# A software-pipelined transformer block on one core: three column-strip products made neighbours, the key product moved ahead of them, the output product moved into the next slot

## The chip, the cores and the metric

One core of a Trainium2 chip runs the whole program. The metric is the device time of one execution in microseconds. Three timed runs of the kernel before gave 581.37, 579.84 and 581.23 us (median 581.23). One more execution was profiled; it took 578.15 us, of which 576.3 us are the span that the trace covers. TensorE's granted clock was 0.996 of full speed over that span.

## The reference, cut to what matters

The input is 32 sequences ("batches" here) of 128 tokens and 128 features, with a conditioning vector each. Everything is float32.

```
y      = clip(modulated_linear(x))                      # per batch
q,k,v  = y@Wq (16 heads of 64), y@Wk, y@Wv (4 groups)
A      = softmax(q k^T / 8) v ;  x1 = x + y + A@Wpost   # attention over 128 tokens
kx     = modulated_linear(x1)  -> 16 heads of 8
mix    = softmax(kx kx^T / sqrt(8)) kx                  # per token, over its 16 heads
tok    = modulated_linear(mix)
out    = x1 + mixture_of_8_experts(tok)                 # top 2, experts over capacity are dropped
```

## The kernel before, in words

The program is written engine by engine; each engine has its own instruction list and waits on semaphores for the others. The first stage, attention and head mixing, is a software pipeline over the 32 batches. It runs in *slots*: in slot s every engine does a part of several batches: a = s+1 (queries, keys, values, the first scores), s (transposed scores, exponentials, denominators, attended values), c = s-1 (output projection of the attention, the key product of head mixing), h = s-2 (head scores), d = s-3 (mixing and its output product). Slots 4 to 29 are a hardware loop over pairs of slots; slots -2 to 3, 30 and 31 and the three drain slots are unrolled. After that comes the mixture of experts, which the change doesn't touch.

The order of the work within a slot is written out by hand in `loop_slot` for TensorE and VectorE, in `slot` for ScalarE and GpSimd. An engine works strictly down its list, so an instruction that waits holds up all that is behind it. All accumulators in PSUM are shared between stages: `bank_s` takes the scores of one head group after the other (`scores`, read by VectorE's `heads_max`) and then their transposed negative maxima; `bank_t` the transposed scores, which ScalarE turns into `prob`; `bank_d` the attention's projection (`posts`) and then the softmax denominators; `bank_a[1]` the key product and its turn (`keys`, `keys_turned`) and then the second half of the attended values (`attend(s, j, 1)`); `misc[1]` the second half of the queries and then mixing (`mixing_turned`, `tokens_made`).

Three products use TensorE in column strips of 32: `denominators` (L687) and the two halves of `attend` (L695). Each issues four matmuls of 512 columns, which the trace shows as eight, because a float32 product goes through in two passes. They work on four strips of the array side by side; the trace writes such a shape as 128*32. The transposed scores (L672, L677) use two row halves of the array (64*128), everything else the whole array.

TensorE's order in a slot is: first half of the queries, transposed maxima (L812), first half of the projection, transposed scores 0 and 1 (L672, L677), keys and values, second half of the projection, transposed scores 2 and 3, scores 0 (L662), `keys`, second half of the queries, scores 1, denominators, the next batch's `y` product (L864), `attend` 0, `keys_turned` (L790), scores 2, `attend` 1, `mixing_turned` (L795), scores 3, `tokens_made` (L799). `attend` 1 waits for ScalarE's `keys_twice` (`kx`), which empties `bank_a[1]`. `tokens_made` waits for ScalarE's `mixing_out` (`mixT`).

VectorE keeps the row maxima of the scores (L300), the normalisation of the attended values by `inv_den` (`normalise`, L308), the residual sum (`attended`, L460), and the head mixing: `weight_sums` (L437), `weighted_rows` (`mix_lo`, L447), `row_sum` (L454), `head_scores` (L407), `head_shift` (L413, L418). GpSimd multiplies `pair` (L1360, the head scores' products), scales `xs` (L1332), adds `y` to `x` (L1344) and does the other half of the mixing, `mix_hi` (product L1348, three sums L1355). All ScalarE instructions have line L1001; they are told apart by their tiles. ScalarE's two copies that mirror the head scores (`head_copies`, the tile `score`) exist before the change too.

## Time and profile before

| | |
|---|---|
| timed runs | 579.84 to 581.37 us, median 581.23 |
| profiled execution | 578.15 us, its span 576.3 us |
| busy share of the span | TensorE 91%, VectorE 70%, ScalarE 70%, GpSimd 53% |
| of 50 to 470 us (420 us) | TensorE 386.7 us busy, VectorE 311.7, ScalarE 309.4, GpSimd 252.2 |
| DMA | 7.2 MB in all, nearly all of it in the first and last 30 us |

The starts of the first transposed-score product of each slot (L672) stand 14.1 to 14.4 us apart from slot 4 on. Starts and durations in a timeline are in microseconds from the start of the span. Matmuls overlap: a product's printed duration holds its way through the array, so the cost of one that isn't waiting is the distance from its start to the next start, and idle time before a matmul is counted from a modelled end. The same holds, by about 0.1 us, for VectorE and ScalarE, whose successive instructions overlap by that much where they don't depend on each other.

### The profile page before, as it was taken

What the parts mean: (1) busy time and instruction counts of PE and PEld (TensorE: products, weight loads), DVE (VectorE), ACT (ScalarE), POOL (GpSimd) and SP (SyncE); (2) the same over time, 40 slices, a digit from 0 to 9 for tenths busy, and PEclk for the clock granted to TensorE, in tenths of its full rate; (3) what the DMA queues carried; (4) which work ended last, traced back from release to release, by engine and by line L of the source; (5) the groups of instructions that cost most, each with busy time, mean ns of one, the idle gap of its engine ahead of it and who ended that gap; (6) DMA issues with size and microseconds to landing.
All of it is one profiled execution on the core that took longest, in us unless ns stands there. A gap on an engine that the chain in (4) does not pass through costs nothing.

```text
span 576.3 us, 12883 instructions
## 1 busy us (share of the span) xinstructions
PE 524.4 (91%) x3896; PEld 349.0 (61%) x3896; DVE 403.7 (70%) x715; ACT 402.9 (70%) x911; POOL 303.6 (53%) x268
## 2 busy tenths in 40 slices
PE   7999999999999999999999999999999987978997
PEld 7755555555556556565656565655565665655665
DVE  4234777777777777777777777777777767962866
ACT  3667677777777777777777777777777644656783
POOL 1002666666666666666666666666666544600951
PEclk9999999999999999999999999999999999999999
DMA  7400000000000000000000000000000000000004
GB/s 237 100 2 2 1 2 0 1 1 0 0 0 0 0 0 0 0 0 0 0 0 0 0 0 0 0 0 0 0 0 0 1 2 0 1 1 2 1 1 146
DMA packets 9365, 7.20 MB, mean 12 GB/s; under 512 B 1088, under 2 KB 8832, under 8 KB 9216
## 3 DMA queue, kind: packets, MB, share of 16 engines
q1 hardware_dynamic: 9344, 6.94, 4.0%
q8 instruction: 11, 0.18, 0.1%
q14 instruction: 10, 0.08, 0.0%
HBM read 4.84 MB, written 2.10 MB: 12 GB/s over the span
## 4 chain that ended last, share of the span: by engine, by line
PE 67%; ACT 17%; issue 8%; DVE 5%; DMA 1%; ACTq 1%; SPq 1%; POOL 0%; DVEq 0%; POOLq 0%
PE misc L702 11%; PE bank_d L710 10%; PE bank_t L677 10%; PE bank_a L695 5%; PE bank_t L947 4%; PE bank_t L672 4%; PE misc L826 3%; ACT inv_den L1001 3%; ACT log_den L1001 3%; PE bank_s L662 3%; PE misc L799 2%; ACT q L1001 2%; PE misc L828 2%; PE bank_s L955 2%; ACT kx L1001 2%
## 5 line engine op out<-in xcount | busy, mean ns | idle before, releaser
L1360 POOL TENSOR_TENSOR pair<-kx 128x1152 f32<-128x1152 f32 x32 | 82.4, 2575 | 182.9 <-DVE shifted L418 165.1
L300 DVE TENSOR_REDUCE row_max<-bank_s 128x4 bf16<-128x512 f32 x128 | 88.5, 691 | 52.0 <-PE bank_s L662 52.0
L695 PE MATMUL bank_a<-prob,v 128*32 128x512 f32 x512 | 68.1, 604 | 24.6 <-ACT kx L1001 24.6
L1355 POOL TENSOR_TENSOR mix_hi<-mix_hi 128x512 f32<-128x512 f32 (+2 forms) x96 | 80.5, 838 | 7.5
L1001 ACT ACTIVATE prob<-bank_t 128x512 f32<-128x512 f32 x128 | 69.5, 594 | 21.4 <-PE bank_t L677 21.4
L1348 POOL TENSOR_TENSOR mix_hi<-weight,kx 128x1024 f32<-128x1024 f32 x32 | 76.7, 2397 | 0.0
L710 PE MATMUL bank_d<-attT,wpost_sb 128*128 128x128 f32 x512 | 70.6, 282 | 0.1
L702 PE MATMUL misc<-yT,wq_sb 128*128 128x128 f32 x512 | 69.1, 278 | 0.7 <-DVE yT L489 0.7
L710 PEld LDWEIGHTS bank_d<-attT,wpost_sb 128*128 128x128 f32 x512 | 65.8, 195 | 2.1 <-issue 0.3
L677 PE MATMUL bank_t<-qT,kT 64*128 64x256 f32 x512 | 65.7, 376 | 0.0
L702 PEld LDWEIGHTS misc<-yT,wq_sb 128*128 128x128 f32 x512 | 62.2, 192 | 3.5 <-issue 2.0
L454 DVE TENSOR_REDUCE mix_part<-mix_lo 128x128 f32<-128x1024 f32 x32 | 63.0, 1968 | 0.3
L677 PEld LDWEIGHTS bank_t<-qT,kT 64*128 64x128 f32 x512 | 49.3, 189 | 4.9
L460 DVE TENSOR_TENSOR x_all<-bank_d,x_all 128x128 f32 (+1 forms) x32 | 9.3, 291 | 59.7 <-PE bank_d L710 59.7
L662 PE MATMUL bank_s<-k,q 128*128 128x256 bf16 x256 | 49.3, 274 | 0.5 <-ACT q L1001 0.3
L1001 ACT ACTIVATE qT<-misc 128x512 f32<-128x512 f32 x64 | 38.1, 595 | 14.0 <-PE misc L702 13.9
L407 DVE TENSOR_REDUCE score<-pair 128x144 f32<-128x1152 f32 x32 | 43.0, 1342 | 2.5 <-POOL pair L1360 2.5
L447 DVE TENSOR_TENSOR mix_lo<-weight,kx 128x1024 f32<-128x1024 f32 x32 | 44.4, 1387 | 0.0
L308 DVE TENSOR_TENSOR attT<-bank_a,inv_den 128x512 f32<-128x512 f32 x64 | 43.4, 679 | 0.0
L1001 ACT ACTIVATE q<-qT 128x512 bf16<-128x512 f32 x64 | 40.3, 629 | 1.1
L1001 ACT ACTIVATE neg_diag<-bank_s 128x512 bf16<-128x512 f32 x32 | 19.1, 597 | 30.6 <-PE bank_s L812 30.6
L662 PEld LDWEIGHTS bank_s<-k,q 128*128 128x128 bf16 x256 | 24.7, 109 | 15.9 <-issue 10.8
(182 smaller groups left out, 954.9 us busy)
## 6 DMA issues: line engine op xcount, KB each, us to landing
out<-acc_all SPq DMA_DIRECT2D x8, 256.0 KB, 2.3
x_all<-in_xT SPq DMA_DIRECT2D x1, 1024.0 KB, 9.3
w_sb<-in_w SPq DMA_DIRECT2D x2, 512.0 KB
x_all<-in_xT SPq DMA_DIRECT2D x1, 768.0 KB, 7.0
wq_sb<-in_wq SPq DMA_DIRECT2D x1, 512.0 KB, 5.4
wpost_sb<-in_wpost SPq DMA_DIRECT2D x1, 512.0 KB, 9.5
x_all<-in_xT SPq DMA_DIRECT2D x1, 256.0 KB, 3.3
b_rows<-in_b SPq DMA_DIRECT2D x16, 4.0 KB
```

Of the source, the lines that this page charges most:

```text
L300: V.tensor_reduce(bass.AP(row_max, first_w * (P + 1) + HPG * p, [[HPG * P, P], [P + 1, 2], [KEY, 2], [1, 1]]), bank_s[:, :, :].rearrange(" ...
L447: V.tensor_tensor(mix_lo[:, :, :].rearrange("p r (h e) -> p r h e", e=MD), weight[:, jd, 0:MH // 2, :].unsqueeze(3).to_broadcast([P, MH // ...
L454: V.tensor_reduce(mix_part[:, :], mix_lo[:, :, :].rearrange("p r f -> p f r"), AX.X, ALU.add).then_inc(s_lo, 3)
L662: last = mm(bank_s[:, 2 * w:2 * w + 2, :], q16[:, j, g // 2, g % 2 * 2 + w, :], k16[:, j, g // 2, :, :], start=(w == 0), stop=True, skip_g ...
L677: last = mm(bank_t[half][:, w:w + 2, :], kT[rows, j, p, :], qT[rows, j, p, w:w + 2, :], start=False, stop=True, skip_group_check=True)
L695: last = mm(bank_a[part][rows, :], v[:, j, g, 32 * part:32 * (part + 1)], prob[:, g, :, :], start=True, stop=True, skip_group_check=True)
L702: last = mm(bank[:, c % 4, :], wq_sb[:, c * P:(c + 1) * P], yT[:, :], start=(c % 4 == 0), stop=True, skip_group_check=True)
L710: last = mm(bank_d[:, 0, :], wpost_sb[:, k, :], attT[:, k, :], start=(k == 0), stop=(k == CHUNKS - 1))
L1001: return nc.scalar.activation(out_, in_, func, **kw)
L1348: G.tensor_tensor(mix_hi[:, jd, :, :].rearrange("p r (h e) -> p r h e", e=MD), weight[:, jd, MH // 2:MH, :].unsqueeze(3).to_broadcast([P, ...
L1355: G.tensor_tensor(mix_hi[:, jd, 0:r, :], mix_hi[:, jd, 0:r, :], mix_hi[:, jd, r:2 * r, :], ALU.add).then_inc(s_hi, 1)
L1360: G.tensor_tensor(pair[:, :, :], bass.AP(kx2, jc * 2 * P, [[4 * P, P], [0, SHIFTS], [1, P]]), bass.AP(kx2, jc * 2 * P, [[4 * P, P], [MD, S ...
```

## The change

It only reorders. No instruction is added or taken away, and no shape changes.

- TensorE: `keys` goes ahead of transposed scores 2 and 3, `keys_turned` ahead of scores 1, and the `y` product ahead of the denominators, so that denominators, `attend` 0 and `attend` 1 are neighbours. Scores 3 go to the next slot, behind the first half of the queries; `tokens_made` goes to the next slot, behind them. The second half of the projection goes up to right behind the transposed maxima.
- VectorE: `heads_max(.., 3)` and the second `normalise` go to the head of the next slot; `attended` ahead of `head_scores`; `heads_max(a, 1)` behind the mixing sums; `yT` ahead of the first `normalise`.
- ScalarE: the first half of the queries is copied ahead of `neg_diag`; `tokens_out` goes to the next slot, and `x1_scaled` directly behind it, ahead of the exponentials; `keys_out` ahead of `v`; `head_copies` ahead of the second half of the queries; `keys_twice` and `y` ahead of its narrowing and of the two denominator instructions, `log_den` and `inv_den`.

```diff
--- before
+++ after
@@ -462,2 +462,6 @@
                 def loop_slot():
+                    if B:
+                        heads_max(s, 3)
+                    if C:
+                        normalise(c, 1)
                     if D:
@@ -465,7 +469,5 @@
                         weighted_rows()
-                    head_scores()
                     if C:
                         attended()
-                    if A:
-                        heads_max(a, 0)
+                    head_scores()
                     if D:
@@ -473,3 +475,3 @@
                     if A:
-                        heads_max(a, 1)
+                        heads_max(a, 0)
                     if D:
@@ -477,9 +479,5 @@
                     mixed(mix_part[:, :])
-                    head_shift()
                     if A:
-                        heads_max(a, 2)
-                    if s_is(s, BATCH - 1):
-                        count_ahead()
-                    if B:
-                        normalise(s, 0)
+                        heads_max(a, 1)
+                    head_shift()
                     if has(a + 1):
@@ -489,5 +487,9 @@
                         V.tensor_scalar(yT[:, :], misc[0][:, 1, :], CLAMP, -CLAMP, ALU.min, ALU.max).then_inc(s_yT, 1)
-                    if A:
-                        heads_max(a, 3)
+                    if s_is(s, BATCH - 1):
+                        count_ahead()
                     if B:
+                        normalise(s, 0)
+                    if A:
+                        heads_max(a, 2)
+                    if s_is(s, BATCH - 1):
                         normalise(s, 1)
@@ -809,2 +811,10 @@
                     if B:
+                        scores(s, j, 3)
+                    if has(d - 1):
+                        tokens_made(d - 1)
+                    if C:
+                        if isinstance(s, int) and c == 0:
+                            pe.wait_ge(s_ld_post, 32)
+                        posts(c, 0)
+                    if B:
                         pe.wait_ge(s_max, 4 * n(s))
@@ -815,5 +825,3 @@
                     if C:
-                        if isinstance(s, int) and c == 0:
-                            pe.wait_ge(s_ld_post, 32)
-                        posts(c, 0)
+                        posts(c, 1)
                     if s_is(s, 0):
@@ -829,6 +837,6 @@
                            stop=True, skip_group_check=True).then_inc(s_kv_mm, 1)
-                    if C:
-                        posts(c, 1)
                     if final:
                         gate_logits(parts_early[1])
+                    if C:
+                        keys(c)
                     if B:
@@ -840,4 +848,2 @@
                         scores(a, ja, 0)
-                    if C:
-                        keys(c)
                     if A:
@@ -849,10 +855,7 @@
                         gate_logits(parts_early[2])
+                        gate_logits(parts_early[3])
+                    if C:
+                        keys_turned(c)
                     if A:
                         scores(a, ja, 1)
-                    if final:
-                        gate_logits(parts_early[3])
-                    if B:
-                        if C:
-                            pe.wait_ge(s_x1T, n(c))
-                        denominators(s)
                     if s_is(s, -1):
@@ -865,8 +868,6 @@
                     if B:
+                        if C:
+                            pe.wait_ge(s_x1T, n(c))
+                        denominators(s)
                         attend(s, j, 0)
-                    if C:
-                        keys_turned(c)
-                    if A:
-                        scores(a, ja, 2)
-                    if B:
                         if C:
@@ -881,5 +882,3 @@
                     if A:
-                        scores(a, ja, 3)
-                    if D:
-                        tokens_made(d)
+                        scores(a, ja, 2)
                     if final:
@@ -891,2 +890,3 @@
                     if s == BATCH:
+                        tokens_made(d - 1)
                         posts(c, 0)
@@ -1131,3 +1131,3 @@
 
-                def mixing_out():
+                def mixing_out(d):
                     act.wait_ge(s_mixT_mm, n(d))
@@ -1137,3 +1137,3 @@
 
-                def tokens_out():
+                def tokens_out(d):
                     act.wait_ge(s_o_mm, n(d))
@@ -1145,2 +1145,3 @@
                     if s == BATCH:
+                        tokens_out(d - 1)
                         copy_logits(EARLY, 4)
@@ -1157,5 +1158,5 @@
                         ahead(0, 1, 2)
-                        mixing_out()
+                        mixing_out(d)
                         ahead(3)
-                        tokens_out()
+                        tokens_out(d)
                     if s == BATCH + 1:
@@ -1164,10 +1165,10 @@
                         ahead(5, 6)
-                        mixing_out()
+                        mixing_out(d)
                         ahead(7)
-                        tokens_out()
+                        tokens_out(d)
                     if s == BATCH + 2:
                         ahead(8)
-                        mixing_out()
+                        mixing_out(d)
                         ahead_keep(9)
-                        tokens_out()
+                        tokens_out(d)
                         ahead_relu(11)
@@ -1181,2 +1182,5 @@
                     return
+                if A:
+                    copy_q(a, ja, 0)
+                    narrow_q(a, ja, 0)
                 if B:
@@ -1185,5 +1189,6 @@
                     f(neg_diag[:, j, :, :], bank_s[:, :, :], scale=-1.0).then_inc(s_neg, 1)
-                if A:
-                    copy_q(a, ja, 0)
-                    narrow_q(a, ja, 0)
+                if has(d - 1):
+                    tokens_out(d - 1)
+                if C:
+                    x1_scaled()
                 if B:
@@ -1199,2 +1204,5 @@
                         f(k16[rows, ja, :, half, :], misc[0][rows, 0:2, :]).then_inc(s_k16, 1)
+                if C:
+                    keys_out()
+                if A:
                     need(act, s_av_mm, 2 * n(a - 2))
@@ -1202,4 +1210,2 @@
                       misc[0][:, 2:4, :].rearrange("p a (g e) -> p (a g) e", e=KEY)).then_inc(s_v, 1)
-                if C:
-                    x1_scaled()
                 if B:
@@ -1207,2 +1213,3 @@
                     exp_scores(s, 3)
+                head_copies()
                 if A:
@@ -1210,8 +1217,3 @@
                 if C:
-                    keys_out()
-                if A:
-                    narrow_q(a, ja, 1)
-                if B:
-                    invert_den(s)
-                head_copies()
+                    keys_twice()
                 if has(a + 1):
@@ -1222,8 +1224,9 @@
                       bias=modb_sb[:, 0:1]).then_inc(s_y_raw, 1)
-                if C:
-                    keys_twice()
+                if A:
+                    narrow_q(a, ja, 1)
+                if B:
+                    invert_den(s)
                 head_weights()
                 if D:
-                    mixing_out()
-                    tokens_out()
+                    mixing_out(d)
```

## Rows read from the trace of the kernel before

**Rows 1.** Timeline of TensorE: start us, us, line, out<-in, [idle before <-releaser].

```profile
252.72 1.06 PE L687 MATMUL bank_d<-prob,ones 128*32 128x512 f32 x8
253.72 0.49 PE L864 MATMUL misc<-xs,modw_sb 128*128 128x128 f32 x2
254.13 1.06 PE L695 MATMUL bank_a<-prob,v 128*32 128x512 f32 x8
...
256.48 1.06 PE L695 MATMUL bank_a<-prob,v 128*32 128x512 f32 x8 [0.80 <-ACT kx L1001]
...
258.37 0.49 PE L799 MATMUL misc<-mixT,modw_sb 128*128 128x128 f32 x2 [0.35 <-ACT mixT L1001]
...
260.86 0.39 PE L672 MATMUL bank_t<-neg_diag,g_rows 64*128 64x512 bf16 x2
...
262.04 0.71 PE L826 MATMUL misc<-yT,wk_sb 128*128 128x128 f32 x4
...
263.02 1.05 PE L710 MATMUL bank_d<-attT,wpost_sb 128*128 128x128 f32 x8
264.01 0.39 PE L672 MATMUL bank_t<-neg_diag,g_rows 64*128 64x512 bf16 x2
```

**Rows 2.** Timeline of TensorE, the last two slots of the pipeline.

```profile
451.98 1.06 PE L687 MATMUL bank_d<-prob,ones 128*32 128x512 f32 x8
452.87 1.04 PE L695 MATMUL bank_a<-prob,v 128*32 128x512 f32 x8
...
459.96 0.39 PE L672 MATMUL bank_t<-neg_diag,g_rows 64*128 64x512 bf16 x2
```

**Rows 3.** Timeline of ScalarE in the same slot as Rows 1.

```profile
262.14 1.09 ACT L1001 ACTIVATE prob<-bank_t 128x512 f32<-128x512 f32 x2 [0.38 <-PE bank_t L677]
263.22 0.38 ACT L1001 ACTIVATE kT<-misc 128x256 f32<-128x256 f32 x1
...
264.69 0.40 ACT L1001 ACTIVATE x1s<-x_all,style 128x128 f32 x1
...
266.74 0.60 ACT L1001 ACTIVATE qT<-misc 128x512 f32<-128x512 f32 x1 [0.36 <-PE misc L702]
...
270.19 0.38 ACT L1001 ACTIVATE kx<-bank_a 128x256 f32<-128x256 f32 x1
```

**Rows 4.** Timeline of VectorE in the same slot.

```profile
258.13 0.69 DVE L300 TENSOR_REDUCE row_max<-bank_s 128x4 bf16<-128x512 f32 x1
258.73 0.68 DVE L308 TENSOR_TENSOR attT<-bank_a,inv_den 128x512 f32<-128x512 f32 x1
259.33 0.57 DVE L437 TENSOR_REDUCE h_den<-weight 128x16 f32<-128x256 f32 x1
259.82 1.50 DVE L447 TENSOR_TENSOR mix_lo<-weight,kx 128x1024 f32<-128x1024 f32 x1
...
264.23 0.29 DVE L460 TENSOR_TENSOR x_all<-bank_d,x_all 128x128 f32 x1 [1.64 <-PE bank_d L710]
...
268.72 0.24 DVE L442 RECIPROCAL h_rden<-h_den 128x16 f32<-128x16 f32 x1
...
269.91 0.58 DVE L413 TENSOR_REDUCE h_max<-score 128x16 f32<-128x256 f32 x1 [0.42 <-ACT score L1001]
270.52 0.43 DVE L418 TENSOR_TENSOR shifted<-score,h_max 128x256 f32<-128x256 f32 x1
```

**Rows 5.** Timeline of GpSimd in the same slot.

```profile
256.90 2.58 POOL L1360 TENSOR_TENSOR pair<-kx 128x1152 f32<-128x1152 f32 x1 [5.29 <-DVE shifted L418]
...
260.20 2.96 POOL L1348 TENSOR_TENSOR mix_hi<-weight,kx 128x1024 f32<-128x1024 f32 x1
```

**Rows 6.** Timeline of GpSimd in the last slot of the pipeline.

```profile
458.77 1.96 POOL L1348 TENSOR_TENSOR mix_hi<-weight,kx 128x1024 f32<-128x1024 f32 x1
460.81 3.47 POOL L1355 TENSOR_TENSOR mix_hi<-mix_hi 128x512 f32<-128x512 f32 x3
```

**Rows 7.** Timeline of VectorE in the last slot of the pipeline.

```profile
458.89 2.92 DVE L447 TENSOR_TENSOR mix_lo<-weight,kx 128x1024 f32<-128x1024 f32 x1
```

More of the change, by code:

```diff
@@ L465, in loop_slot @@
                         weighted_rows()
-                    head_scores()
                     if C:
                         attended()
+                    head_scores()
+                    if D:
+                        row_sum()
                     if A:
@@ L471, in loop_slot @@
                     if D:
-                        row_sum()
+                        weight_inverses()
+                    mixed(mix_part[:, :])
                     if A:
                         heads_max(a, 1)
-                    if D:
-                        weight_inverses()
-                    mixed(mix_part[:, :])
                     head_shift()
-                    if A:
-                        heads_max(a, 2)
-                    if s_is(s, BATCH - 1):
-                        count_ahead()
-                    if B:
-                        normalise(s, 0)
                     if has(a + 1):
@@ L881, in loop_slot @@
                     if A:
-                        scores(a, ja, 3)
-                    if D:
-                        tokens_made(d)
+                        scores(a, ja, 2)
                     if final:
@@ L1210, in slot @@
                 if C:
-                    keys_out()
-                if A:
-                    narrow_q(a, ja, 1)
-                if B:
-                    invert_den(s)
-                head_copies()
+                    keys_twice()
                 if has(a + 1):
@@ L1222, in slot @@
                       bias=modb_sb[:, 0:1]).then_inc(s_y_raw, 1)
-                if C:
-                    keys_twice()
+                if A:
+                    narrow_q(a, ja, 1)
+                if B:
+                    invert_den(s)
                 head_weights()
                 if D:
-                    mixing_out()
-                    tokens_out()
+                    mixing_out(d)
             slots(act, slot)
```

## The prediction

> **What bounds the kernel now.** I read the busy shares first, then the timeline of one slot on each engine, then the chain of waits. TensorE is the busiest engine by far, and in the slot shown it stands idle at two places only: 0.80 us before the second half of `attend`, ended by ScalarE's `kx`, and 0.35 us before `tokens_made`, ended by `mixT` [rows 1]. The chain of waits runs through TensorE for the whole slot except at these two places. So the slot is TensorE's own work plus two waits. From one slot's first L672 to the last slot's there are 14 slots: (459.96 - 260.86)/14 = 14.22 us each [rows 1, 2].
>
> The reader should see three costs in TensorE's rows. First the two waits. Second, switching between strips and the whole array: denominators to the `y` product takes 1.00 us (252.72 to 253.72) and `y` to `attend` 0.41 us for two short passes [rows 1]. In slot 30, which has no `y` product, the same denominators are followed directly by `attend` after 0.89 us [rows 2]. Third, nothing else: after 256.48 the rest is dense.
>
> **The change on TensorE.** No matmul is added or removed.
>
> - Strips in a row: denominators and `attend` 0 each pass to another strip product in 0.89 us instead of 1.00, 0.22 together. The `y` product's 0.41 contains a way back into strips and a weight load that stood open; I put it at 0.25, so 0.16 less. Sum about 0.4 us.
> - `keys` and its turn ahead: between `keys_turned` and `attend` 1 now lie scores 1, `y`, the denominators and `attend` 0 where only scores 2 lay, so `kx` has emptied `bank_a[1]` by then. That takes the 0.80 us wait.
> - `tokens_made` one slot later, behind the queries: the 0.35 us wait goes. `tokens_out` follows it on ScalarE, where it stands behind `neg_diag`.
>
> TensorE's own slot would then be 14.22 - 0.80 - 0.35 - 0.4 = 12.7 us. Idle time is counted from modelled ends, so each wait may be worth 0.1 to 0.2 us more: 12.3 to 12.7. I take this as the floor and not as the forecast, since the change makes new waits.
>
> **The new loop.** Scores 3 of a batch now run at the head of the next slot, and they wait for `heads_max(.., 2)`. On VectorE that one stands behind the first `normalise`, which needs `inv_den`. On ScalarE the two denominator instructions are now almost last. Behind scores 3 TensorE queues tokens, projection, maxima, second half of the projection, and then the transposed scores that start ScalarE's next run of exponentials. That closes a loop through all three engines. I add it up from the start X of the first exponential.
>
> - ScalarE's run, where it should never wait: two exponentials to `kT` 1.08 us (262.14 to 263.22). `kT`, two `k`, `v`: in the old order 1.47 us until `x1s` starts, which itself waited for the residual sum; I take 1.40. Two more exponentials 1.09 less an overlap of 0.10. The remaining nine instructions (second query copy, `kxT`, narrowing, `log_den`, `inv_den`, two mirror copies, `y`, `kx`) are the same nine that run without idle time between 266.74 and 270.57 now: 3.83 us [rows 3]. Sum 7.30 us from X to the end of `inv_den`.
> - VectorE: from there to the start of `normalise` 0.12 (two waits; estimate between the smallest distance seen, 0.03, and the 0.16 at `attended`). `normalise` to `heads_max` 0.60, `heads_max` itself 0.69 [rows 4].
> - TensorE: 0.05 to start, scores 3 take 0.43 to their end (estimate: two matmuls of 256 columns, their load open because they waited), 0.04 back to VectorE.
> - VectorE: `heads_max` 3 then the second `normalise`, 0.60 and 0.68 [rows 4].
> - TensorE: 0.05, then the second half of the projection: 0.99 from its start to L672 (263.02 to 264.01) plus 0.10 for an open load [rows 1].
> - L672 to the next first exponential: 260.86 to 262.14 = 1.28 [rows 1, 3].
>
> 7.30 + 0.12 + 0.60 + 0.69 + 0.05 + 0.43 + 0.04 + 0.60 + 0.68 + 0.05 + 1.09 + 1.28 = 12.93 us. That is above TensorE's floor, so the three-engine loop sets the period.
>
> **What else lies near.** `x1_scaled` now stands in front of the exponentials, so a late residual sum delays all of ScalarE. Its path: second `normalise` 0.60, `h_den` 0.49, `mix_lo`, `attended`, `x1s` [rows 4]. The start of `mix_lo` is wanted at X + 7.30 + 0.12 + 0.60 + 0.69 + 0.05 + 0.43 + 0.04 + 0.60 + 0.60 + 0.49 = X + 10.92. Here GpSimd matters. In the last slot `mix_hi` ran 458.77 to 460.73 and `mix_lo`, wanted at 458.89, ended at 461.81: it took 2.92 us instead of about 1.1, that is, it waited for `mix_hi` to end and then ran 1.08 us [rows 6, 7]. In the slot of rows 5, `mix_lo` started first with 1.50 and `mix_hi` took 2.96 instead of 1.96 [rows 4 to 6]. The one that comes second waits for the whole instruction.
>
> So where is GpSimd at X + 10.92? Scores 0 start at L672 + 1.18 + 0.98 (262.04 to 263.02) + 0.3 for `keys` and the switch + 1.18 for the second transposed pair = L672 + 3.64 = X + 2.36 [rows 1]; `heads_max` 0 at X + 2.8; 0.60; then from `h_rden` to `h_max` 1.19 less 0.42 of idle time, 0.77; `heads_max` 1 0.60; `h_max` to `shifted` 0.61; `shifted` 0.43 [rows 4]: its end at X + 5.8. `pair` follows 0.08 later and `mix_hi` 3.30 us after it (256.90 to 260.20) [rows 5], at X + 9.2, ending at X + 11.15, with the first of its sums 0.08 behind, at X + 11.2 [rows 6]. `mix_lo` comes within `mix_hi`, waits till X + 11.15, ends at X + 12.23. `attended` (overlap 0.08, 0.29 long), 0.17 to `x1s` (264.52 to 264.69), 0.30 more to the exponential [rows 3, 4]: X + 12.91. The two paths tie, and the period stays 12.9 us, with a margin of 0.3 us before the first sum of `mix_hi` would get in ahead of `mix_lo`.
>
> **Moves costed at nothing.** `neg_diag` behind the query copies: the two instructions of 0.6 us [rows 3] end before the maxima come, since these wait for scores 3. `heads_max` 1 behind the mixing sums: it is wanted by scores 2 only, some 3 us later. `yT` is early by the length of the first `normalise`. `tokens_out` and its `misc[1]`: the second query product comes some 6 us after it. If one of these covers goes, its own 0.3 to 0.6 us join the period. The SP queue and all DMAs are untouched; nothing that moves issues one. GpSimd's list is unchanged, only its releases move.
>
> **Sum.** Slots 4 to 31 are 28 slots at 14.22 - 12.93 = 1.29 us: 36 us. The fill is less loaded and the drain is another order of the same work; I take 1 us gained there, with 3 either way. 578.15 - 37 = 541.2 us for an execution like the profiled one. The timed runs before lay 1.7 to 3.2 us above the profiled one; taking 1.8 of that, the forecast is 543 us.
>
> **Rivals.**
>
> - *TensorE is the bound (0.07).* If the loop is 0.3 to 0.6 us shorter than I add it up, TensorE's 12.3 remain: 28 x 1.92 = 54 us, 526 us. For it: I took two open loads and upper ends. Against it: ScalarE's 7.30 us are nearly all read from dense rows.
> - *Sums of `mix_hi` ahead of `mix_lo`, in every slot (0.13).* If `mix_lo` is wanted after X + 11.2, the first sum holds it off. That sum is about half of the three (3.47 less 1.00 of waiting for `mix_lo`) [rows 6, 7], 1.3 us. `mix_lo` then ends at X + 13.6 and the next X comes at X + 14.28. The period is 14.28 against 14.22: with the 1 us of the fill this is no change, 582 us. Every tenth by which `shifted` is later than X + 5.8 adds 2.8 us; from 0.05 us later on, the kernel is slower than before by over 0.3%, at 0.2 later 588 us. It decides at a delay of 0.3 us on the path to `mix_lo`, about the size of my estimates' error. The Trainium skill, "SBUF — State Buffer", section "Who interferes with whom", says that a VectorE instruction with two SBUF inputs and a GpSimd instruction that reads SBUF exclude each other for their whole length, the later one blocking. Rows 4 to 7 agree (2.92 us for 1.1), and by that rule alone, whichever is issued first decides between 12.9 and 14.3 us.
> - *The same in one of the two slots of the loop body (0.13).* The two already differ before. Mean period 13.6: 28 x 0.62 = 17 us, 563 us.
> - *The forecast's case (0.62)*, period 12.7 to 13.3, 533 to 550 us. The rest (0.05) are longer loops of another kind, between 550 and 575.
>
> About 0.3% is what a measurement of this kernel can tell. The 0.13 of the second rival splits into 0.02 faster, 0.06 same, 0.05 slower; one more in a hundred goes to slower. Faster 0.88, same 0.06, slower 0.06. The range 532 to 566 holds the forecast's case and the half-blocked one and leaves out TensorE's floor and the fully blocked loop.
>
> **What would show it.** Right: L687, L695, L695 at distances of 0.89 us; no idle time before L695; a TensorE wait of about half a microsecond ended by `row_max` before scores 3, and a short one ended by `attT` before the second half of the projection; ScalarE without idle time from the first exponential to `inv_den`; `mix_lo` at 1.1 to 1.6 us; L672 some 12.9 us apart. Wrong: `mix_lo` at 2 us or more with `mix_hi`'s sums beside it, an idle ScalarE in front of `x1s`, or TensorE dense with L672 at 12.3.

## The result, and the profile after

The changed kernel takes 537.69 us (median of four runs, 536.6 to 538.42) where the kernel before takes 580.71 (four runs, 579.84 to 581.37): a ratio of 0.926, 95% interval 0.924 to 0.928. The forecast was 543 us, range 532 to 566. The profiled execution took 537.94 us, against the 541.2 that the sum gave for it. One execution of 1719 us of the kernel of experiment 7, and one of 852 us of the kernel before beside experiment 12, are left out of the medians and ratios.

The two profiled executions lie 40.2 us apart. The starts of the first transposed-score product of each slot (L672 before, L674 after) show where that came from. From slot 4 to slot 31 there are 27 distances. They were 14.23 us on average and are (421.78 - 75.52)/27 = 12.82 now: 27 x 1.41 = 38.0 us. The rest after the last of them shrank from 116.3 to 114.3 us, and slot 4 starts 0.1 us earlier. So the gain is the period of the loop.

The page of after, busy shares and clock:

```profile
PE 509.7 (95%) x3896; PEld 359.1 (67%) x3896; DVE 405.6 (76%) x715; ACT 385.1 (72%) x911; POOL 299.8 (56%) x268
...
PEclk9999999999999999999999999999999989989999
```

Every engine has as many instructions as before; they stand in a shorter span. TensorE's idle time in the span fell from 51.9 us (576.3 - 524.4) to 26.4 (536.1 - 509.7), and its busy time by 14.7 us. Now the timeline of TensorE in after, to be held against [rows 1, 2]:

```profile
247.92 1.07 PE L689 MATMUL bank_d<-prob,ones 128*32 128x512 f32 x8
248.80 1.90 PE L697 MATMUL bank_a<-prob,v 128*32 128x512 f32 x16
250.63 0.33 PE L797 MATMUL misc<-ident,mix 128*128 128x128 f32 x1
...
252.38 0.39 PE L664 MATMUL bank_s<-k,q 128*128 128x256 bf16 x2 [0.31 <-DVE row_max L300]
...
254.15 1.16 PE L712 MATMUL bank_d<-attT,wpost_sb 128*128 128x128 f32 x8
255.24 0.39 PE L674 MATMUL bank_t<-neg_diag,g_rows 64*128 64x512 bf16 x2
```

Denominators to `attend` takes 0.88 us, and both halves of `attend` are one run of 16 with nothing in front: the wait for `kx` is gone. So is the wait for `mixT`. In their place stands 0.31 us before scores 3, ended by `row_max`, and the second half of the projection at 254.15, whose weight load waited 0.21 us for `attT`: 1.09 us from there to L674 (255.24), as the sum had it.

ScalarE and VectorE of after in the same slot [rows 3, 4]:

```profile
243.85 1.06 ACT L1001 ACTIVATE prob<-bank_t 128x512 f32<-128x512 f32 x2
...
250.23 0.63 ACT L1001 ACTIVATE inv_den<-log_den 128x512 f32<-128x512 f32 x1
...
256.43 0.40 ACT L1001 ACTIVATE x1s<-x_all,style 128x128 f32 x1 [1.25 <-DVE x_all L460]
256.73 1.06 ACT L1001 ACTIVATE prob<-bank_t 128x512 f32<-128x512 f32 x2
```

```profile
250.95 0.69 DVE L308 TENSOR_TENSOR attT<-bank_a,inv_den 128x512 f32<-128x512 f32 x1 [1.20 <-PE bank_a L697]
251.56 0.69 DVE L300 TENSOR_REDUCE row_max<-bank_s 128x4 bf16<-128x512 f32 x1
252.81 0.70 DVE L300 TENSOR_REDUCE row_max<-bank_s 128x4 bf16<-128x512 f32 x1 [0.56 <-PE bank_s L664]
253.41 0.68 DVE L308 TENSOR_TENSOR attT<-bank_a,inv_den 128x512 f32<-128x512 f32 x1
254.01 0.58 DVE L437 TENSOR_REDUCE h_den<-weight 128x16 f32<-128x256 f32 x1
254.51 1.55 DVE L447 TENSOR_TENSOR mix_lo<-weight,kx 128x1024 f32<-128x1024 f32 x1
255.98 0.28 DVE L460 TENSOR_TENSOR x_all<-bank_d,x_all 128x128 f32 x1
```

And GpSimd [rows 5, 6]:

```profile
249.70 2.58 POOL L1363 TENSOR_TENSOR pair<-kx 128x1152 f32<-128x1152 f32 x1 [4.05 <-DVE shifted L418]
...
253.00 1.97 POOL L1351 TENSOR_TENSOR mix_hi<-weight,kx 128x1024 f32<-128x1024 f32 x1
255.06 3.48 POOL L1358 TENSOR_TENSOR mix_hi<-mix_hi 128x512 f32<-128x512 f32 x3
```

Read these from the end. ScalarE's exponentials at 256.73 don't start 1.28 us behind L674 (255.24) as in [rows 1, 3], but 1.49 behind it. They stand behind `x1s` at 256.43, which waits for `attended` (255.98), which stands behind `mix_lo`. `mix_lo` is wanted at 254.51 and takes 1.55 us. `mix_hi` is at work until 254.97, and the first of its sums starts at 255.06. So the residual sum, and not the transposed scores (L674) alone, sets the next slot's start.

### The profile page after: what moved, and what is told of

It is laid out like the page before. It is cut to its first block, busy times and chain, and to the rows that moved or that the text cites. A ratio compares the mean times of both kernels' runs of the same rounds, so it can differ in the third digit from the quotient of the medians.

```text
span 536.1 us, 12857 instructions
## 1 busy us (share of the span) xinstructions
PE 509.7 (95%) x3896; PEld 359.1 (67%) x3896; DVE 405.6 (76%) x715; ACT 385.1 (72%) x911; POOL 299.8 (56%) x268
## 4 chain that ended last, share of the span: by engine, by line
PE 51%; ACT 16%; DVE 15%; issue 13%; DVEq 1%; ACTq 1%; POOL 1%; POOLq 0%
PE bank_d L712 6%; PE bank_t L679 6%; PE bank_a L697 6%; ACT prob L1001 6%; PE bank_s L664 4%; PE bank_t L947 4%; DVE row_max L300 4%; PE misc L704 4%; PE bank_d L689 3%; PE bank_t L674 2%; DVE attT L308 2%; DVE mix_lo L447 2%; PE bank_s L955 2%; PE bank_d L955 2%; PE bank_a L635 2%
## 5 line engine op out<-in xcount | busy, mean ns | idle before, releaser
L1358 POOL TENSOR_TENSOR mix_hi<-mix_hi 128x512 f32<-128x512 f32 (+2 forms) x96 | 104.9, 1092 | 7.5
L704 PE MATMUL misc<-yT,wq_sb 128*128 128x128 f32 x512 | 67.8, 276 | 0.3 <-DVE yT L487 0.3
L712 PEld LDWEIGHTS bank_d<-attT,wpost_sb 128*128 128x128 f32 x512 | 62.1, 192 | 7.1 <-DVE attT L308 7.1
L1351 POOL TENSOR_TENSOR mix_hi<-weight,kx 128x1024 f32<-128x1024 f32 x32 | 63.0, 1970 | 0.0
L697 PE MATMUL bank_a<-prob,v 128*32 128x512 f32 x512 | 62.4, 606 | 0.0
L454 DVE TENSOR_REDUCE mix_part<-mix_lo 128x128 f32<-128x1024 f32 x32 | 61.4, 1918 | 0.3
L664 PE MATMUL bank_s<-k,q 128*128 128x256 bf16 x256 | 49.6, 275 | 8.1 <-DVE row_max L300 7.6
L447 DVE TENSOR_TENSOR mix_lo<-weight,kx 128x1024 f32<-128x1024 f32 x32 | 47.8, 1495 | 0.0
L697 PEld LDWEIGHTS bank_a<-prob,v 128*32 128x32 f32 x512 | 17.0, 111 | 38.7 <-issue 37.9
L1001 ACT ACTIVATE x1s<-x_all,style 128x128 f32 (+1 forms) x32 | 12.8, 401 | 38.9 <-DVE x_all L460 38.9
L664 PEld LDWEIGHTS bank_s<-k,q 128*128 128x128 bf16 x256 | 19.6, 103 | 27.9 <-ACT k L1001 10.3
```

The lines of the kernel that those rows point to most:

```text
L447: V.tensor_tensor(mix_lo[:, :, :].rearrange("p r (h e) -> p r h e", e=MD), weight[:, jd, 0:MH // 2, :].unsqueeze(3).to_broadcast([P, MH // ...
L454: V.tensor_reduce(mix_part[:, :], mix_lo[:, :, :].rearrange("p r f -> p f r"), AX.X, ALU.add).then_inc(s_lo, 3)
L664: last = mm(bank_s[:, 2 * w:2 * w + 2, :], q16[:, j, g // 2, g % 2 * 2 + w, :], k16[:, j, g // 2, :, :], start=(w == 0), stop=True, skip_g ...
L697: last = mm(bank_a[part][rows, :], v[:, j, g, 32 * part:32 * (part + 1)], prob[:, g, :, :], start=True, stop=True, skip_group_check=True)
L704: last = mm(bank[:, c % 4, :], wq_sb[:, c * P:(c + 1) * P], yT[:, :], start=(c % 4 == 0), stop=True, skip_group_check=True)
L712: last = mm(bank_d[:, 0, :], wpost_sb[:, k, :], attT[:, k, :], start=(k == 0), stop=(k == CHUNKS - 1))
```

## The experiments

Each ratio is against the kernel before, run on the same chip beside it; after stands at 0.926. "Period" is the mean distance of the first L674 (or L672) of a slot, slots 4 to 31: 14.23 before, 12.82 after. X is the start of a slot's first exponential, as in the prediction. "The port" stands for what `mix_lo` on VectorE and `mix_hi` on GpSimd can't have at the same time [rows 4 to 7]. The port path is the one from `shifted` through `pair`, `mix_hi`, `mix_lo`, `attended` and `x1s` to the next exponentials; the other path is the one through `inv_den` and scores 3. Line numbers differ by a few between the kernels.

**1. `mix_hi` held behind `mix_lo`: is the port path the one that binds?** The kernel is after, with GpSimd's `mix_hi` made to wait for `mix_lo` in every slot but the drain's.

```diff
+                    if not isinstance(s, int) or s < BATCH:
+                        pool.wait_ge(s_lo, 4 * d + 1)
```

> The kernel after, with GpSimd's product mix_hi made to wait until VectorE has written mix_lo of the same batch. Theory P (port): in the kernel after the period of 12.84 us is set by mix_lo waiting for the end of mix_hi (254.51 to 254.97), then attended, x1s and the first exponential. With mix_lo alone on the port it ends 0.46 us earlier; the path through inv_den then sets the period, 12.67 us, and the time falls by 28 x 0.17 = 5 us, to about 533. L672 to the first exponential goes from 1.49 to 1.28 us. Theory T (TensorE bounds the slot) and theory I (the path through inv_den bounds it): no change, 537 to 538, or a little slower where mix_hi is now late for the mixing sums.

535.27 us, ratio 0.922 (0.917 to 0.927), period 12.77, where 533 us and 12.67 were expected. The interval overlaps that of after, so the time alone doesn't tell the two apart; the period does. VectorE and GpSimd of this kernel:

```profile
243.04 1.22 DVE L447 TENSOR_TENSOR mix_lo<-weight,kx 128x1024 f32<-128x1024 f32 x1
...
249.09 0.29 DVE L395 TENSOR_TENSOR mix_sum<-mix_part,mix_hi 128x128 f32<-128x128 f32 x1 [0.37 <-POOL mix_hi L1360]
```

```profile
244.34 1.97 POOL L1353 TENSOR_TENSOR mix_hi<-weight,kx 128x1024 f32<-128x1024 f32 x1 [2.30 <-DVE mix_lo L447]
```

`mix_lo` takes 1.22 us instead of 1.55, but the period falls by 0.06 only. The exponentials come 1.28 and 1.37 us behind L674 in turn, so the path through the port is off. What it leaves is the other path, the one through `inv_den`, and that one got longer: the exponentials now start earlier against TensorE's work, from the exponentials to `kT` it is 1.08 and 0.99 us in turn instead of 0.96, and `inv_den` ends at X + 7.15 and X + 7.06 instead of X + 7.01. VectorE's new wait of 0.37 us for the sums of `mix_hi` costs nothing: `normalise`, further down its list, still waits for `inv_den` or the attended values. So the two paths lie 0.06 us per slot apart, the port's the longer: nearly the tie that was forecast.

**2. `mix_hi` and its sums ahead of `xs` and `x + y`: what if a sum gets in first?**

```diff
-                if A:
-                    pool.wait_ge(s_yT, n(a))
-                if has(s + 2):
-                    xs_of(s + 2, j)
-                if A:
-                    G.tensor_tensor(x_all[:, col(a)], x_all[:, col(a)], yT[:, :], ALU.add).then_inc(s_xy, 1)
```

(The same lines follow behind the sums of `mix_hi`.)

> The kernel after, with GpSimd's mix_hi and its three sums put ahead of xs and x+y in its list. mix_hi then starts some 0.8 us earlier and its first sum is issued before mix_lo is wanted. Theory P: mix_lo waits for that sum of 1.3 us instead of for mix_hi, takes 2.2 us instead of 1.55, and the period becomes 13.4 us: about 555 us. Theories T and I: no change, since no engine has more work, 538.

551.53 us, ratio 0.951 (0.946 to 0.956), period 13.41, as expected (13.4). GpSimd and VectorE:

```profile
247.47 1.97 POOL L1345 TENSOR_TENSOR mix_hi<-weight,kx 128x1024 f32<-128x1024 f32 x1
249.53 3.47 POOL L1352 TENSOR_TENSOR mix_hi<-mix_hi 128x512 f32<-128x512 f32 x3
```

```profile
249.75 2.13 DVE L447 TENSOR_TENSOR mix_lo<-weight,kx 128x1024 f32<-128x1024 f32 x1
```

`mix_lo` is wanted 0.22 us behind the start of the first sum and takes 2.13 us: it waits out the rest of that sum. Up to there nothing moved: `inv_den` ends at X + 7.01 and `mix_lo` is wanted at X + 10.66, both as in after. In after it comes 0.55 us ahead of the first sum (254.51 and 255.06). That distance is what stands between the measured kernel and this one.

**3. Scores 3 at the head of the slot.** They run ahead of the first queries.

```diff
+                    if B:
+                        scores(s, j, 3)
                     if A:
                         pe.wait_ge(s_yT, n(a))
                         queries(a, 0)
-                    if B:
-                        scores(s, j, 3)
```

> The kernel after, with scores 3 ahead of the first half of the queries on TensorE, so that the 0.9 us of queries no longer lie in the shadow of the wait for row_max but behind it. Theory I (the path inv_den, normalise, heads_max, scores 3, heads_max, normalise, projection is within 0.2 us of the bound): the projection comes 0.7 us later, the period grows by 0.5 us to 13.3, about 551 us. Theory T (only TensorE's amount of work counts): no change, 538.

553.6 us, ratio 0.954 (0.949 to 0.959), period 13.39, as expected (13.3). TensorE:

```profile
262.47 0.39 PE L664 MATMUL bank_s<-k,q 128*128 128x256 bf16 x2 [1.27 <-DVE row_max L300]
```

The wait for `row_max`, 0.31 us in after, is 1.27 without the queries in front, and the queries then come late for what follows. What ends the wait doesn't move: `heads_max` 2 stands behind `normalise`, and that behind `inv_den`. The exponentials follow L674 by 1.28 and 1.37 us here, so the port path is off, and this is the loop of the prediction, seen from its TensorE end.

**4. The strips torn apart again.** Scores 2 run between the two halves of `attend`.

```diff
                         attend(s, j, 0)
+                    if A:
+                        scores(a, ja, 2)
+                    if B:
                         if C:
                             pe.wait_ge(s_kx2, n(c))
                         attend(s, j, 1)
...
-                    if A:
-                        scores(a, ja, 2)
```

> The kernel after, with scores 2 put back between attend 0 and attend 1, so that the strips are two in a row and one apart. TensorE pays one more way out of and into strips, some 0.2 to 0.3 us a slot. Theory L (the loop through all engines bounds, TensorE has 0.5 us of waits a slot): the extra cost shortens the wait for row_max before scores 3, no change, 537 to 539 us. Theory T: 28 x 0.25 = 7 us more, 545 us.

538.77 us, ratio 0.930 (0.925 to 0.935), period 12.83: no change that can be told from after. TensorE:

```profile
262.37 1.04 PE L697 MATMUL bank_a<-prob,v 128*32 128x512 f32 x8
263.34 0.39 PE L664 MATMUL bank_s<-k,q 128*128 128x256 bf16 x2
263.66 1.07 PE L697 MATMUL bank_a<-prob,v 128*32 128x512 f32 x8
```

Two more switches between strips and the whole array cost 0.24 us: from the first `attend` to the mix's turn are 264.66 - 262.37 = 2.29 us with scores 2 among them; in after it is 250.63 - 248.80 = 1.83, and scores 2 are 0.22 more (250.80 to 251.02 there). They are paid out of TensorE's wait before scores 3, which has gone in this trace. In the kernel as changed, having strips side by side gives nothing of itself.

**5. ScalarE's second narrowing behind the denominators.** It moves behind `log_den` and `inv_den`, so that these come earlier.

```diff
-                if A:
-                    narrow_q(a, ja, 1)
...
+                if A:
+                    narrow_q(a, ja, 1)
```

> The kernel after, with ScalarE's narrowing of the second half of the queries behind the two denominator instructions, so that inv_den ends 0.52 us earlier. Theory P (port): mix_lo is then wanted earlier but still waits for the end of mix_hi, which depends on shifted and pair only; the period stays 12.8 us and the time 537 to 539. Theory I (the path through inv_den sets the period): 0.4 to 0.5 us less a slot, 524 to 527 us.

537.25 us, ratio 0.925 (0.921 to 0.929), period 12.83: no change. `inv_den` ends 0.52 us earlier (X + 6.49), and the period doesn't follow. TensorE and VectorE:

```profile
252.39 0.38 PE L664 MATMUL bank_s<-k,q 128*128 128x256 bf16 x2
```

```profile
241.46 1.73 DVE L447 TENSOR_TENSOR mix_lo<-weight,kx 128x1024 f32<-128x1024 f32 x1
...
254.52 1.58 DVE L447 TENSOR_TENSOR mix_lo<-weight,kx 128x1024 f32<-128x1024 f32 x1
```

Not all of the 0.52 us reaches `mix_lo`. Scores 3 (L664 at 252.39) no longer wait for `row_max`, but TensorE's own row gets to them no sooner, so `mix_lo` is wanted at X + 10.39 instead of 10.58 in one slot, and at X + 10.65, as in after, in the other. Where it is wanted earlier it takes longer (1.73 us for 1.55), because it waits for the same end of `mix_hi`. So what comes off the path through `inv_den` is worth nothing: the port path binds alone.

**6. Both, 1 and 5.** The edit is that of 1 and that of 5.

> Both edits together: mix_hi waits for mix_lo, and the narrowing stands behind the denominators. If the two paths (port, and inv_den) are in parallel and each near 12.8 us, neither edit alone gives much and both together give the 0.52 us: period 12.77 - 0.42 = 12.35, where TensorE's own work begins to bound, about 523 us. If one of the two paths was no bound at all, the result is that of the better single edit, 535 us.

531.34 us, ratio 0.913 (0.909 to 0.916), period 12.67 (12.54 and 12.80 in turn). It is the fastest kernel of the study, 6.3 us under after, but the 523 us expected weren't reached: they took TensorE's floor, 12.35 a slot. No idle time of a matmul set is left between 100 and 420 us that another engine ends. Three rows of the slot of 12.80 us, and two of the waits of that stretch (what waited, for what: us in total, times, longest):

```profile
248.50 0.33 PE L797 MATMUL misc<-ident,mix 128*128 128x128 f32 x1
248.85 0.39 PE L664 MATMUL bank_s<-k,q 128*128 128x256 bf16 x2
249.32 1.15 PE L704 MATMUL misc<-yT,wq_sb 128*128 128x128 f32 x8
```

```profile
PEld bank_s L664 <- ACT q L1001: 4.6, 24, 0.2
PEld misc L704 <- issue: 3.9, 11, 0.4
```

L797 to scores 2 takes 0.35 us (0.31 in the other slot), 0.17 in after (250.63 to 250.80): with the narrowing behind the denominators, the weight load of scores 2 waits for `q`, 24 times. Scores 2 to the queries takes 0.47 us, 0.22 in after; no data is late, and it comes 11 times, in every second slot, where the loop body of two slots begins anew. In after both lie in front of a wait for `row_max` and cost nothing. The 0.25 us is the difference of the two slots (12.80 and 12.54), and 12.54 less some 0.17 for `q` is near the 12.35. That these two make up the miss is read from the rows; no kernel without them was run.

**7. From the kernel before, the tokens alone one slot later.**

```diff
+                    if has(d - 1):
+                        tokens_made(d - 1)
                     if B:
                         pe.wait_ge(s_max, 4 * n(s))
...
-                    if D:
-                        tokens_made(d)
```

(`tokens_out` on ScalarE moves likewise, behind `neg_diag`.)

> The kernel before, with tokens_made and tokens_out of a batch one slot later and nothing else. The wait for mixT (0.35 us and an open load of 0.11) goes from TensorE's row. Theory S (in the kernel before each TensorE wait adds to the slot): 28 x 0.46 = 13 us less, about 568 us. Rival: kx is then as late as before against an earlier TensorE and the wait before attend 1 grows by the same amount: no change, 580.

577.08 us, ratio 0.995 (0.991 to 0.998), where 568 was expected; the distances are 14.03 us, but for the last (15.45). The wait for `mixT` [rows 1] is gone; another one is there:

```profile
255.29 1.06 PE L695 MATMUL bank_a<-prob,v 128*32 128x512 f32 x8 [0.80 <-ACT kx L1002]
...
257.07 1.16 PE L702 MATMUL misc<-yT,wq_sb 128*128 128x128 f32 x8 [0.24 <-DVE yT L489]
```

```profile
256.14 0.68 DVE L308 TENSOR_TENSOR attT<-bank_a,inv_den 128x512 f32<-128x512 f32 x1
256.74 0.28 DVE L489 TENSOR_SCALAR yT<-misc 128x128 f32<-128x128 f32 x1
```

Without the tokens in front, the queries start 1.78 us behind `attend` 1 instead of 2.22 (256.48 to 258.70 before), and by the row would start 0.24 us earlier still: `yT` stands behind `heads_max` 2 and `normalise` on VectorE, and is ready 1.73 us behind `attend` 1 in both kernels.

**8. The same with `yT` ahead of the first `normalise`.**

```diff
-                    if B:
-                        normalise(s, 0)
                     if has(a + 1):
                         dve.wait_ge(s_y_raw, n(a + 1))
...
+                    if B:
+                        normalise(s, 0)
```

> The kernel before with tokens_made one slot later, as in tokens_alone, and VectorE's yT ahead of the first normalise, as in the kernel after. In tokens_alone the queries then waited 0.24 us for yT, which stood behind heads_max 2 and that normalise. Theory S2 (the wait for mixT was exchanged for the wait for yT): with yT 0.6 us earlier the slot loses the whole 0.46 us, period 13.75, about 567 us. Rival (something else holds the slot at 14.03): no change against tokens_alone, 576.

562.77 us, ratio 0.971 (0.966 to 0.975), period 13.62, somewhat better than expected (567 us, 13.75). One of TensorE's waits is left between 100 and 420 us:

```profile
PE bank_a L695 <- ACT kx L1002: 18.5, 23, 0.8
```

That is 14 us more than 7 from one instruction's place: in the change, the new place of `yT`, which the prediction had put among the moves at nothing, is a condition for the gain of the tokens. The earlier `yT` without the later tokens wasn't run; in the kernel before no matmul waits for `yT`. The wait for `kx` that is left, 0.80 us, is what still lies between this kernel and after: 13.62 - 12.82 = 0.80.

**9. From the kernel before, strips alone.** The denominators move behind the `y` product, so that these and `attend` 0 are neighbours.

```diff
-                    if B:
-                        if C:
-                            pe.wait_ge(s_x1T, n(c))
-                        denominators(s)
...
+                    if B:
+                        if C:
+                            pe.wait_ge(s_x1T, n(c))
+                        denominators(s)
                     if B:
                         attend(s, j, 0)
```

> The kernel before, with the y product ahead of the denominators, so that denominators and attend 0 are neighbours. TensorE saves 0.11 + 0.16 us a slot there, but its next wait, for kx before attend 1, is behind it. Theory W (the saved time is lost in that wait, and the denominators are 0.2 us later for ScalarE): no change, 579 to 584 us. Theory T (fewer changes between strips and the whole array give their time): 7 us less, 573 us.

585.67 us, ratio 1.008 (1.005 to 1.011): slower, where no change was expected (579 to 584 us). TensorE:

```profile
246.59 1.06 PE L695 MATMUL bank_a<-prob,v 128*32 128x512 f32 x8 [1.25 <-ACT kx L1001]
```

The wait for `kx` [rows 1] grew from 0.80 to 1.25 us and took all that the switches gave, and 0.1 us more: the distances are 14.24 and 14.50 in turn, before 14.13 and 14.38. The 0.1 us is ScalarE's: the denominators come later, `inv_den` ends at X + 7.32 instead of 7.21, and `kx` stands behind it. Beyond that, three of the 31 distances were 15.87 us, see the last section.

**10. After, with the tokens back in their own slot.**

```diff
-                    if has(d - 1):
-                        tokens_made(d - 1)
...
+                    if D:
+                        tokens_made(d)
```

(`tokens_out` likewise.)

> The kernel after with tokens_made at the end of its own slot again. TensorE waits 0.5 us for mixT there, and the queries and scores 3 come 0.4 us later than the wait for row_max ends now. The path through inv_den, scores 3 and the second normalise grows by 0.37, to 12.67 + 0.37 = 13.04 us; the port path stays at 12.84. About 543 us. If the later slot of the tokens were worth its whole wait, 12.84 + 0.6: 554 us; if nothing, 538.

557.94 us, ratio 0.961 (0.957 to 0.964), where 543 was expected; distances of 13.96 and 13.35 in turn. VectorE and GpSimd show why:

```profile
252.09 1.22 DVE L447 TENSOR_TENSOR mix_lo<-weight,kx 128x1024 f32<-128x1024 f32 x1
...
265.44 2.27 DVE L447 TENSOR_TENSOR mix_lo<-weight,kx 128x1024 f32<-128x1024 f32 x1
```

```profile
252.20 3.59 POOL L1355 TENSOR_TENSOR mix_hi<-mix_hi 128x512 f32<-128x512 f32 x3
...
265.36 3.47 POOL L1355 TENSOR_TENSOR mix_hi<-mix_hi 128x512 f32<-128x512 f32 x3
```

In one slot `mix_lo` starts 0.11 us ahead of the first sum and takes 1.22; in the next it is wanted 0.08 behind it and takes 2.27. It is wanted at X + 11.02 and X + 11.33 in turn, where after has X + 10.58 and X + 10.66; the expectation had given 0.37 us of delay to the path through scores 3 and none to the race. From exponential to exponential it is 13.04 and 14.30 us. This is the half-blocked loop of the prediction's third rival (12.93 and 14.28), with its period (13.6) and nearly its time (563).

**11. After, with the `y` product between the denominators and `attend` 0.** The denominators move ahead of it.

```diff
+                    if B:
+                        if C:
+                            pe.wait_ge(s_x1T, n(c))
+                        denominators(s)
...
                     if B:
-                        if C:
-                            pe.wait_ge(s_x1T, n(c))
-                        denominators(s)
                         attend(s, j, 0)
```

> The kernel after with the y product between the denominators and attend 0, where it was before. Its switches cost TensorE 0.27 us, as much as in scores2_between, which changed nothing. But the product ends 0.6 us later, and on ScalarE y stands in front of the narrowing, log_den and inv_den. Theory Q (it is the queue on ScalarE that counts): those three are 0.5 us later, period 13.2 to 13.3, 548 to 551 us. Theory W (a TensorE slot has room for it, nothing else matters): 538 us.

576.19 us, ratio 0.991 (0.988 to 0.994), period 14.10; 548 to 551 was expected. ScalarE, VectorE and GpSimd:

```profile
256.44 0.43 ACT L1002 ACTIVATE misc<-misc,modb_sb,demod 128x128 f32<-128x128 f32 x1 [0.49 <-PE misc L871]
```

```profile
262.13 2.28 DVE L447 TENSOR_TENSOR mix_lo<-weight,kx 128x1024 f32<-128x1024 f32 x1
```

```profile
262.06 3.47 POOL L1359 TENSOR_TENSOR mix_hi<-mix_hi 128x512 f32<-128x512 f32 x3
```

The copy of `y` waits 0.49 us with the denominators queued behind it, `inv_den` ends at X + 7.61 instead of X + 7.01, and `mix_lo` falls 0.07 us behind the first sum, now in both slots. 0.6 us of delay became 1.3 us of period. From exponential to exponential it is 14.14 and 14.21 us: the second rival (14.28).

**12. The same with the edit of 1.** The edits are those of 11 and of 1: without the port, is only the delay left?

> y_between with one edit more: GpSimd's mix_hi waits for mix_lo, as in lo_first. In y_between inv_den came 0.60 us later than in the kernel after, and the period grew by 1.3 us. Theory P2 (the delay itself costs some 0.55 us a slot, and the rest is that mix_lo now comes 0.07 us behind the first sum of mix_hi and waits 1.2 us for it): with the order on the port fixed the period is 12.77 + 0.55 = 13.3 us, about 550 us, 26 us less than y_between. Rival (the whole 1.3 us comes from ScalarE's and TensorE's queues): 574 to 576 us, no change against y_between.

553.52 us, ratio 0.955 (0.952 to 0.958), period 13.34, as expected (13.3; the time is 3.5 us above the 550); `mix_lo` takes 1.21 us. So 0.76 of the 1.28 us that 11 lost per slot are the lost race for the port, and 0.52 are the delay of `inv_den`. TensorE waits up to 0.6 us for `row_max` in this kernel, so the two more switches that the `y` product costs it there don't show in the period.

## Why the prediction was right

**The three-engine loop.** It closed as described, and the marks named for "right" are in the rows of after; only the wait for `row_max` is 0.31 us where about half a microsecond was named. One mark named for "wrong" is there too: ScalarE stands idle in front of `x1s`, 1.25 us, where it didn't before [rows 3]. The mark tells less than it was meant to: the idle time is 1.98 and 2.07 us in the blocked loop of experiment 11, but with the port path off (experiment 1) it is still 0.90 and 0.99. The terms of the loop came out so: ScalarE's run 7.01 us (250.86 - 243.85) where 7.30 was summed, the one term that was over-sized by more than 0.1; `inv_den` to `normalise` 0.09 for 0.12; `normalise` to `heads_max` 0.61 for 0.60; the projection 1.09 for 1.09. With 1.28 us from L674 to the exponentials, where the port path made it 1.49, these terms give 12.88 - 0.21 = 12.67 us. With the port path off in truth (experiment 1) it is 12.77, since ScalarE's run is 7.15 and 7.06 us there. So the sum of 12.93 was 0.16 too long, by ScalarE's term.

**The port path.** It was summed at 12.91 and is 12.88 in this slot, and it is the one that binds; the sum called it a tie. Its points against X: end of `shifted` 5.71 (5.8 forecast), `mix_hi` 9.15 (9.2), its first sum 11.21 (11.2), `mix_lo` wanted 10.66 (10.92) and ended 12.21 (12.23). Experiment 5 ends `inv_den` 0.5 us earlier and gains nothing; experiment 1 takes the port off and gains 0.06 us per slot, since the other path then holds. The over-sized 7.30 did the forecast no harm: as long as `mix_lo` comes within `mix_hi`, the port path doesn't depend on that term. It did make the margin ahead of the first sum 0.3 us; it is 0.55. With a margin of 0.3 the two blocked loops looked nearer than they were.

**The rivals.** TensorE as the bound didn't come; even experiment 6, where no matmul set stands idle for another engine, has 12.67 us and not 12.3. (It reached the 12.7 that the prediction had worked out first.) The fully and the half-blocked loop didn't come in after, but experiments 11 and 10 are these two, with periods near those forecast for them (14.10 and 13.63, against 14.28 and 13.6). Each came of one product put elsewhere on TensorE, which took 0.6 us of the margin ahead of the first sum (from 0.55 us ahead to 0.07 and 0.08 behind). The Trainium skill, "SBUF — State Buffer", section "Who interferes with whom", has the later of the two instructions block for the whole length of the other. The rows agree: 1.21 to 1.22 us alone, 1.55 behind the rest of `mix_hi`, 2.13 to 2.28 behind nearly the whole of a sum.

**The strips.** The floor of 12.7 counted 0.4 us for fewer switches: that term has no part in the result. The distances came as read (0.88), but in after they shorten only an engine that waits anyway (experiment 4), and from the kernel before they went into a longer wait for `kx` (experiment 9). The gain is that of the two waits removed. The tokens' part of it (experiment 8, 13.62 against 14.23) needs the earlier `yT` (experiment 7). The part of `kx` wasn't run alone; it is read from the difference of 0.80 us that is left between experiment 8 and after, which is as long as the wait.

**Moves costed at nothing.** None was run alone, but in after the only wait of a matmul between 100 and 420 us is that for `row_max`, and `neg_diag` itself waits 0.73 us for the maxima, so none shows a cost. The exception is `yT`, whose earlier place was worth 0.4 us per slot to the queries.

**Fill and drain.** 1 us was taken, 2.1 was gained; 27 distances and not 28 lie between slots 4 and 31. Of the 5.3 us between the forecast of 543 and the measured 537.69, 3.3 are the sum's (541.2 against 537.94). The other 2 are the step from a profiled execution to the timed ones: 1.8 us was added for it, and this time the timed median lies 0.25 us under the profiled execution.

## What to carry to other kernels

Add up every loop that passes through several engines from one instruction's start back to its own next start, and do it to the second one too: the distance from the longest path to the second is all that you gain by mending the longest (0.06 us a slot in experiment 1). Where two engines exclude each other, ask which of the two instructions comes first and by what margin, since half a microsecond of delay anywhere ahead of it can cost more than twice itself. When an edit removes a wait, look at what the engine asks for next and where that stands in its own queue: here one instruction's place was worth 14 us.

## What was not expected of the hardware

**The clock of TensorE in experiment 9.** Windows of that kernel from 262 to 268 us, the columns: length, busy share and count of TensorE, weight loads, VectorE, ScalarE, GpSimd, then the granted clock:

```profile
262.00:263.00 1.00, 0.65 (x8) 0.29 (x4) 1.00 (x4) 0.38 (x2) 1.00 (x1) 1.00 0.00 0
263.00:264.00 1.00, 1.00 (x5) 1.00 (x6) 1.00 (x3) 0.15 (x1) 1.00 (x1) 0.54 0.00 0
264.00:265.00 1.00, 1.00 (x7) 1.00 (x7) 1.00 (x2) 0.30 (x1) 1.00 (x4) 0.50 0.00 0
...
266.00:267.00 1.00, 1.00 (x8) 0.95 (x7) 1.00 (x1) 0.97 (x3) 1.00 (x1) 0.76 0.00 0
267.00:268.00 1.00, 1.00 (x12) 0.78 (x10) 0.18 (x1) 0.60 (x1) 0.92 (x2) 1.00 0.00 0
```

From 263 us on the granted clock was at the lower of its two levels (1.2 GHz, not 2.4), and by 267 it was back. Ahead of the fall TensorE had stood idle 1.24 us for `kx`, until `attend` 1 at 261.07, and 0.35 us for `mixT`, until 262.96; in the last microsecond before it TensorE was busy for 0.65 us. Three of 31 distances had such a fall and were 15.87 us instead of 14.24: 4.9 of the 11 us by which this profiled execution, 589.23 us, lay above the one of before. Some 3 us more are the 0.1 us of every slot, and 3 the fill and the drain. In the other slots the same two waits left the clock where it was; why it fell in these three isn't shown. The timed runs of experiment 7 look alike: four of the nine have a mean granted clock of 0.982 to 0.985 and took 579.2 to 580.2 us, the other five have 0.991 to 0.994 and took 574.2 to 577.1.

**The small gaps.** Two instructions of GpSimd that depend on each other stand some 0.08 us apart (254.97 to 255.06 in after), and that is enough for a waiting VectorE instruction to get in: `mix_lo` ends 1.09 us behind the end of `mix_hi`, and the first sum, 1.27 us long in the kernel before, takes 2.13. Experiment 10 shows the race at its closest: 0.11 us ahead is 1.22 us, 0.08 behind is 2.27.

**The loop's way back.** In experiment 6, 0.47 us instead of 0.22 between two products of TensorE at the turn of the loop, where nothing hides it: 0.25 us for two slots. In the kernel before, the distances were 14.13 and 14.38 in turn. There `tokens_made` (L799) to the transposed maxima (L812) takes 1.22 us in one slot (258.37 to 259.59) and 1.45 in the next (272.51 to 273.96), with the queries that begin the loop body between them. That is 0.23 of the 0.25 us.
